# State-space stage: output projection in three and four pieces, other products of TensorE's plan moved by a few units

## The reference, cut to what matters

```
# state-space part
xc, z = split(xn @ in_proj.T)                  # "xz": 8 tiles of 128 rows, 4 for xc, 4 for z
xs    = silu(conv4(xc) + conv_b)               # "cv": 4 taps
dt_r, B, C = split(xs @ x_proj.T)              # "xd"
dt    = softplus(dt_r @ dt_proj.T + dt_b)      # "dt"
h[t]  = exp(dt * A) * h[t-1] + dt * B * xs     # scan over time, 512 channels x 16 states
y     = (sum_s h * C + xs * D_skip) * silu(z)
x1    = x + y @ out_proj.T + ffn(xn)           # "out"
# ffn: three layers with weights of +1 and -1
ffn   = s2 * (relu(s1 * (relu(s0 * ([xn, -xn] @ k0)) * 2) @ k1) * 2) @ k2    # "l1", "l2", "l3"
```

## Time and profile before

| | us |
|---|---|
| median of 3 runs | 3573.45 (3572.59 to 3575.95) |
| the profiled execution | 3574.84 |
| its span, first to last instruction | 3573.1 |
| TensorE busy | 3336.7 (93%) |
| VectorE busy | 2739.0 (77%) |
| ScalarE busy | 2221.9 (62%) |
| GpSimd busy | 1517.7 (42%) |

### The profile page before, as it was taken

One profiled execution on the slowest core, in us unless ns is written; L12 is line 12 of the kernel. 1 busy time (PEld: TensorE's weight loads), 2 busy tenths in 40 slices (PEclk: granted clock), 3 DMA queues, 4 the chain that ended last, 5 costly groups with the idle time before them and its releaser, 6 DMA issues. The chain is left out here.

```text
span 3573.1 us, 59783 instructions
## 1 busy us (share of the span) xinstructions
PE 3336.7 (93%) x19726; PEld 1391.0 (39%) x19727; DVE 2739.0 (77%) x4922; ACT 2221.9 (62%) x3475; POOL 1517.7 (42%) x1881
## 2 busy tenths in 40 slices
PE   8998999999999999999999999866999999999987
PEld 5564666643333333333333333252343343343333
DVE  5654223568988988898898898374899999899897
ACT  3331211137777777777777777845777777777773
POOL 2225000003233333333332323313888888888885
PEclk9999999989999999999999999977999999999998
DMA  4443111111111111110111110041222222222221
GB/s 154 132 155 111 45 45 44 41 37 40 47 35 33 37 37 34 31 31 26 32 34 34 33 32 26 12 136 51 63 80 69 75 80 69 75 80 71 72 77 51
DMA packets 160887, 211.62 MB, mean 59 GB/s; under 512 B 32324, under 2 KB 108364, under 8 KB 160604
## 3 DMA queue, kind: packets, MB, share of 16 engines
q1 hardware_dynamic: 141340, 172.51, 15.8%
q0 software_dynamic: 8512, 18.76, 1.7%
q10 hardware_dynamic: 10752, 16.78, 1.4%
HBM read 154.48 MB, written 52.69 MB: 58 GB/s over the span
## 5 line engine op out<-in xcount | busy, mean ns | idle before, releaser
L1270 ACT ACTIVATE prob<-psS 128x1024 f32<-128x1024 f32 (+3 forms) x1280 | 1100.2, 906 | 332.8 <-PE psS L1437 326.8
L1329 DVE TENSOR_REDUCE pmax<-psR 128x1 f32<-128x512 f32 x1674 | 1060.8, 684 | 139.1 <-PE psR L1384 100.1
L1384 PE MATMUL psR<-kslab,qslab 48*128 48x512 bf16 (+3 forms) x2480 | 675.4, 353 | 55.6 <-DVE pmax L1329 23.0
L2097 POOL TENSOR_TENSOR hc<-h_d,crep 128x512 f32<-128x512 f32 x512 | 647.1, 1271 | 181.7 <-DVE h_d L2324 129.8
L1437 PE MATMUL psS<-qslab,kslab 51*128 51x512 bf16 (+3 forms) x2560 | 638.0, 351 | 5.1 <-ACT prob L1270 4.4
L1452 PE MATMUL psVo<-prob,vaug 128*32 128x512 f32 (+3 forms) x5120 | 625.6, 544 | 0.9 <-ACT ov L1274 0.9
L1202 POOL TENSOR_SCALAR_AFFINE_SELECT prob<-prob 128x256 f32<-128x256 f32 (+1 forms) x512 | 208.7, 420 | 774.8 <-ACT prob L1270 774.5
L2324 DVE TENSOR_TENSOR_SCAN h_d<-a,state,psU 128x512 f32<-128x512 f32 x384 | 489.4, 1275 | 0.0
L1384 PEld LDWEIGHTS psR<-kslab,qslab 48*128 48x128 bf16 x2480 | 181.8, 94 | 789.6 <-DVE pmax L1329 461.7
L2314 DVE TENSOR_TENSOR psU<-dtx,psX 128x512 f32<-128x512 f32 x512 | 356.1, 695 | 115.3 <-PE psX L2469 37.6
L2229 ACT ACTIVATE a<-dt,a_neg 128x512 f32<-128x512 f32 x512 | 366.8, 723 | 55.1 <-DVE h_d L2324 53.7
(11 more groups left out here) (299 smaller groups left out, 4875.0 us busy)
## 6 DMA issues: line engine op xcount, KB each, us to landing
crep<-c_rows_d SPq DMA_DIRECT2D x256, 256.0 KB, 3.1
x_e<-rows_d SPq DMA_DIRECT2D x72, 128.0 KB, 2.0
y_d<-y SPq DMA_DIRECT2D x72, 128.0 KB, 1.7
q_d<-parts SPq DMA_DIRECT2D x48, 128.0 KB, 2.4
k_d<-parts SPq DMA_DIRECT2D x48, 128.0 KB, 4.3
qslab<-q_d SPq DMA_DIRECT2D x60, 96.0 KB
kslab<-k_d SPq DMA_DIRECT2D x60, 96.0 KB
x<-in_L_attn_x_dram SPq DMA_DIRECT2D x8, 512.0 KB, 6.1
```

The source lines that it names most:

```text
L1270: act.activation(prob[g % BUFS][:, :, off:BLK], psS[g % 2][:, :, off:BLK], ACT.Exp).then_inc(prob_ready, 1)
L1329: dve.tensor_reduce(into[:, lo:lo + (count - 1) * NEXT + 1:NEXT], psR[at % BANKS][:, 0:count * w].rearrange("p (n w) -> p n w", w=w), AX.X ...
L1384: ins = pe.matmul(dst[:, m * w:(m + 1) * w], qslab[u][rows, i * P:(i + 1) * P], kslab[u][rows, ch * BLK:ch * BLK + w], start=(m == 0), sto ...
L2097: pool.tensor_tensor(hc[:, g % CR], h[:, g % HR], crep[:, g // PAIR % SPR], ALU.mult).then_inc(hc_ready, 1)
```

## The change

All of it is in the table `pieces`. For blocks 1 to 7 `out` 0 is cut into 4, 3 and 3 matmuls at units 6 to 8 instead of 5 and 5 at 6 and 7; `out` 1 into 3, 3, 2 and 2 at units 10 to 13 instead of 5 and 5 at 9 and 10. `l1` 4 to 7 move from units 11, 13, 15, 16 to 12, 15, 16, 17, and `xz` 2 and 3 from 12 and 14 to 14 and 21. In every block `l2` 4 is cut 5, 4, 4, 3 and `l2` 5 to 7 into fours over four units instead of 6, 5, 5 over three, and `xz` 4 and 5 move from units 48 and 52 to 50 and 54. The buffers that `places()` gives follow from the table, and so do the units in which ScalarE, VectorE and GpSimd do their parts.

```diff
--- before.py
+++ after.py
@@ -1902,7 +1902,7 @@
                     done += count
                 assert done == OPS[kind]
 
-            for f, at in enumerate((0, 2, 5, 7, 11, 13, 15, 16) if blk else (0, 2, 8, 9, 10, 11, 12, 13)):
+            for f, at in enumerate((0, 2, 5, 7, 12, 15, 16, 17) if blk else (0, 2, 8, 9, 10, 11, 12, 13)):
                 put("l1", f, at, [4])
             for c in range(PAIR):
                 put("dt", PAIR + c, 1 + 2 * c, [1])
@@ -1910,17 +1910,17 @@
                 for n in range(CT):
                     put("z0", CT + n, 4 + n, [KD])
             if blk:
-                put("out", 0, 6, [5, 5])
-                put("out", 1, 9, [5, 5])
+                put("out", 0, 6, [4, 3, 3])
+                put("out", 1, 10, [3, 3, 2, 2])
             put("l2", 0, 18, [4, 4, 4, 4])
             for f in range(1, 4):
                 put("l2", f, 17 + 5 * f, [5, 4, 4, 3])
             for f, at in enumerate((37, 41, 45, 49)):
-                put("l2", 4 + f, at, [6, 5, 5])
+                put("l2", 4 + f, at, [4, 4, 4, 4] if f else [5, 4, 4, 3])
             put("l3", 0, 53, [6, 7, 6, 7, 6])
             put("l3", 1, 58, [7, 6, 7, 6, 6])
             if blk + 1 < NBLK:
-                for e, at in enumerate(((4, 9, 12, 14) if blk else (14, 15, 16, 17)) + (48, 52, 56, 60)):
+                for e, at in enumerate(((4, 9, 14, 21) if blk else (14, 15, 16, 17)) + (50, 54, 56, 60)):
                     put("xz", e, at, [2])
                 for c, at in enumerate((17 if blk else 19, 23, 28, 33)):
                     put("cv", c, at, [1, 1, 1, 1])
```

## The result

The changed kernel takes 3588.97 us (median of 6 runs, 3586.68 to 3590.56) against 3573.05 (6 runs): ratio 1.0043, 95% interval 1.003 to 1.0056. It is 15.9 us slower; the forecast was 3572 with a range to 3581. The profiled executions took 3588.77 and 3574.84, spans 3587.0 and 3573.1.

A forecast was written before the change was run, and what follows sets the result against it. TensorE was taken to bound blocks 1 to 6; terms -0.8 - 0.6 - 5 x 0.15 + 2 x 0.87 gave -0.4 us, -3.4 without the `l2` 0 wait. It took -1.5: 3572, range 3568 to 3577 (8 in 10: 3563 to 3581).

The forecast's parts named there:

- the clock still falls, 0.90 in that window: Around block starts: TensorE's clock falls despite a shorter `dt` 2 wait; slow matmuls there priced at 1.4 us.
- only what TensorE rests at the seam can be won: Whole stage: TensorE keeps the same work; only its rest around block starts is winnable, and two `psW` waits take it back.
- Rival (b): Block starts: TensorE arrives later and its waits no longer lower the clock; 3564, or 3562 without the `l2` 0 wait; 15%.
- Rival (d): Inside blocks: new small rests make the clock fall a second time, 1.4 us x 6, giving 3580; 5%.
- the load moved out of units 6 to 11 comes back at 22 and 24: Load returns in units 16, 17, 21; VectorE stalls 0.3 us at unit 22 and 1.66 at 24.
- `xz` 1 inherits the 0.5 us wait: Unit 9: `xz` 1 takes the `psW` buffer `out` 1 waited 0.51 us for; wait stays, about 0.6 us.
- `dt` 2 waits less: Block start: TensorE arrives later, so its wait at `dt` 2 is 1.7 us instead of 2.4.
- blocks 1 and 5 start with less lead: After blocks 0 and 4 the next block's spreads have 0.87 us less lead; +0.87 us each.
- the ledger: Per pair of units, lead of spreads over `input_term` gains 3.99 us and loses 1.37 plus load; stalls total 5.67 against 5.81.
- Rival (a): Units 8 to 11: the 3.4 us of stalls are won and nothing returns; 20 us gain, 3553; 8%.
- The wait at `l2` 0: Unit 18: `l2` 0 waits 0.5 us (bounds 0.2 to 1.5) for the `psW` buffer of `l1` 7, paid at unit 22.
- Block 0's -0.8: Block 0, which gets only the second part of the change, gains 0.8 us.

The follow-up runs named there:

- gate28_nowait: after_gate28 with `l1` 5, 6, 7 one unit earlier and `xz` 2 one later, so `l2` 0 no longer takes a just-left buffer; 3564.27 us.
- before_gate28: Kernel before, with ScalarE's `silu_gate` moved from unit 62 of the block before to unit 28 of its own; 3567.05 us.
- after_gate28: Changed kernel, with ScalarE's `silu_gate` moved from unit 62 of the block before to unit 28 of its own; 3570.63 us.
- after_filler: Changed kernel, with the spreads issued at units 0 and 2 of blocks 1 to 7 repeated 8 and 4 times; 3572.41 us.
- early_half: Kernel before with the first half of the change alone (`out`, `l1` 4 to 7, `xz` 2 and 3); 3589.57 us, ratio 1.0046.
- before_shift4: Kernel before with four extra ScalarE copies once, ahead of the stage's first `decay`; 3577.95 us, ratio 1.001.
- after_shift4: Changed kernel with four extra ScalarE copies once, ahead of the stage's first `decay`; 3589.24 us, ratio 1.0038.

## Why the prediction was wrong

**What failed.** The step "the clock still falls, 0.90 in that window", priced at the 1.4 us a seam that it cost before, and the conclusion that only what TensorE rests at the seam can be won. I took the fall at a seam as a fixed price. It is the largest term: with the falls at the seams of blocks 1 to 6 removed on both sides, by the gate's move, the change costs 3.6 us, so 12.3 of the 15.9 are put to the clock. Blocks 1, 2 and 3 had their low stretch grow from 3.5 to 10 us, at some 3 us a block, and block 4, which had none, got one (1.5 us). Before block 7, where I put 0, it grew as well, from 3.4 to 10.2 us, and the block took 1.5 us more. Rival (b) had the clock at the seam as the thing that could move, and the wrong sign: shorter waits did not bring a better clock. It took a wait of 1.25 us at `dt` 2 for short enough, from block 4 alone; in the changed kernel that block has the same 1.25 us wait, and the clock fell. Rival (d) had the sign, 3580, but put the new fall within the block, where the clock stayed at 1.00.

**The sum of the runs.** Evened loads -2.8 (`gate28_nowait` against `before_gate28`), the `psW` wait of `l2` 0 +6.4 (`after_gate28` against `gate28_nowait`), the clock at the seams +12.3: 15.9. The last term is what is left, so that the sum comes out proves nothing; the first two hold with the gate moved, and for a table in which `l1` 5 to 7 and `xz` 2 stand elsewhere too. The intervals of the ratios are 3.6 to 4.6 us to either side, wider than the -2.8, though the slowest execution of `gate28_nowait` (3565.65) is under the fastest of `before_gate28` (3565.82). `after_filler` gives the clock's part independently: the fill took 16.6 us from the changed kernel and 3.5 from the kernel before, 13.1 between them. By either count the clock's part is over three quarters of the loss.

**What was right.** That TensorE is the bound and that the load moved out of units 6 to 11 comes back at 22 and 24: 1.66 was forecast for unit 24, and 1.65 came (1.78 less 0.13). That `xz` 1 inherits the 0.5 us wait. That `dt` 2 waits less, 1.85 instead of 2.40 (1.7 forecast), and that blocks 1 and 5 start with less lead: block 5, whose low stretch stayed short, lost 1.5 us, and the ledger with the wait of 0.86 gives 1.1. Rival (a) was rightly small: nothing of the 3.4 us stayed won in the blocks of the changed kernel.

**What was mis-sized.** The wait at `l2` 0: 0.5 forecast, 0.86 measured, and some 4 us in all (6.4 with the gate moved) instead of 3. The steps not seen were GpSimd's read of the `relu` buffer and three pairs of copies in a row on ScalarE. Block 0's -0.8 was -0.2, since there `l2` 5 waits 0.73 us for `xd`. A short seam was priced at 1.4 us; the fill made blocks 1 to 3 of the kernel before 1.0 to 1.3 us shorter. The forecast's -1.5 was itself a choice between the sum, -0.4, and -3.4 without the wait. Without the clock it met +3.6, 5 us too low, and within the range; that says little for it, since the fall of the clock was part of the forecast.

**What stays open.** Why a given seam is long. In `early_half` seams with the same work before and in them had 3.5, 10 or 13.6 us at the low level, and the seam before block 1 had 10.1 in `before_shift4` and 3.4 in the kernel before with the same waits, so where a seam falls in time plays a part; `after_shift4` moved the blocks by 0.6 to 0.8 us and changed nothing. One regularity is in the traces. Eight of the kernels here have a clock that falls at the seams, which gives 24 seams before blocks 2, 3 and 6. In six of them the low level began 1.8 to 2.9 us after the block's first scan and lasted 10.2 or 13.7 us; in eighteen it began 3.3 to 4.1 us after it and lasted 3.4. The seams before blocks 1, 4 and 7 don't all follow it (3.5 us and 10.2 before block 1 of the changed kernel). No run here isolates the cause. The short seams of the kernel before are no luck of one execution: of its 80 executions on record 78 took 3571.8 to 3576.4 us, and two 3579.2 and 3580.3, at a mean granted clock of 0.976 instead of 0.978. Whether another small change of the table would lose them as this one did, no run tells.

## What to carry to other kernels

A fall of TensorE's clock had no fixed price per wait here: look at the granted clock of each place where the bound engine rests, count the places where it could stay low longer, and put that into the range on the slow side. When a table of work is moved, check each buffer's handover for the emptying time of its last user (1.29 us in the earlier trace rows) and for what its emptier has queued. And first ask whether the rest itself can go: moving one ScalarE function out of the seam and keeping the handovers apart (`gate28_nowait`) gave 3564.3 us, 0.28% under the kernel before and 0.7% under the changed one.

## What the runs showed of the hardware

Twelve repeated matmuls in each of seven seams, about 18 us of added TensorE work, made the changed kernel 16.6 us faster; the granted clock was 1.00 at the seams of blocks 1 to 6. A wait of 2.40 us at `dt` 2 came with 3.5, 10.1 or 13.6 us at 1.2 GHz in one and the same execution (`early_half`). A wait of 1.25 us there, with one of 0.75 behind it, left the clock at 1.00 before block 4 of the kernel before and came with 3.4 us at 1.2 GHz in the changed one. In the Trainium skill (TensorE: Matmul & The Clock Gate, "A second HAM failure mode: psum-queue depth-cycling") brief rests between groups of matmuls over PSUM buffers are told to make the clock swing. The trace agrees at the seams; within the blocks single rests of 0.5 to 1.2 us (0.51 and 0.69 in the changed kernel, 1.19 in `after_gate28`) left it at 1.00.
